# Two one-column operations for a half-mean, and another order of two adds, in a fused spectral convolution kernel

## The reference

```python
def L0(x):                                   # applied to _gn(x)
    X = jnp.fft.rfftn(x, axes=(-2, -1))
    Yr = rconv(Xr, wr) - rconv(Xi, wi) + b_real
    Yi = rconv(Xr, wi) + rconv(Xi, wr) + b_imag
    return jnp.fft.irfftn(lax.complex(Yr, Yi), axes=(-2, -1))
x = x + L0(_gn(x))
x = x + mean_filter_15x15(_gn(x))
```

## Time and profile before

| | |
|---|---|
| median of 3 runs | 4029.41 us (4027.86 to 4030.45) |
| the profiled execution | 4030.95 us |
| its span | 4028.9 us |
| PE busy | 3515.2 us (87%) |
| DVE busy | 3445.0 us (86%) |
| POOL busy | 2638.3 us (65%) |
| ACT busy | 2382.8 us (59%) |
| mean granted clock of TensorE | 0.962 |

### The profile page before, as it was taken

One profiled execution on the slowest core, in us unless ns is written; L12 is line 12 of the kernel. 1 busy time (PEld: TensorE's weight loads), 2 busy tenths in 40 slices (PEclk: granted clock), 3 DMA queues, 4 the chain that ended last, 5 costly groups with the idle time before them and its releaser, 6 DMA issues.

```text
span 4028.9 us, 122552 instructions
## 1 busy us (share of the span) xinstructions
PE 3515.2 (87%) x42592; PEld 2538.7 (63%) x42592; DVE 3445.0 (86%) x6382; ACT 2382.8 (59%) x3774; POOL 2638.3 (65%) x2177
## 2 busy tenths in 40 slices
PE   3199889998999989899798998999898998999988
PEld 1166576665766667666675666666576665766667
DVE  7889977998779978899788997789977998789976
ACT  0078733886248852588427883288733886248852
POOL 5088853887538865588546885388853986538865
PEclk8599999999999999999999999999999999999999
DMA  6511166111741128311382114711165111741114
GB/s 161 169 43 53 44 173 178 52 53 34 225 135 52 52 57 245 91 51 52 100 239 57 51 53 141 208 45 53 42 184 167 52 52 38 222 134 51 52 53 137
DMA packets 228530, 407.91 MB, mean 101 GB/s; under 512 B 98160, under 2 KB 173520, under 8 KB 215888
## 3 DMA queue, kind: packets, MB, share of 16 engines
q1 hardware_dynamic: 205776, 285.88, 24.6%
q10 hardware_dynamic: 22400, 117.46, 10.9%
HBM read 256.31 MB, written 146.80 MB: 100 GB/s over the span
## 4 chain that ended last, share of the span: by engine, by line
PE 52%; DVE 21%; issue 11%; POOL 8%; ACT 5%; ACTq 1%; DVEq 1%; SPq 1%; DMA 0%; POOLq 0%
PE h_ps L658 14%; PE p L549 11%; PE h_ps L453 9%; PE p L684 6%; PE p L491 4%; POOL ob_all L1306 3%; DVE arena L1104 3%; DVE ob_all L1152 3%; DVE half_row L1171 3%; PE xt_ps L443 3%; DVE img L1161 2%; POOL ob_all L1308 2%; POOL arena L1299 2%; DVE ob_all L1231 2%; ACT arena L727 1%
## 5 line engine op out<-in xcount | busy, mean ns | idle before, releaser
L549 PE MATMUL p<-arena,bd_all 64*64 64x512 f16 x16896 | 1206.4, 379 | 30.0 <-DVE ob_all L1152 29.6
L1299 POOL TENSOR_TENSOR arena<-arena 128x512 f16<-128x512 f32 x512 | 594.1, 1160 | 495.7 <-ACT arena L760 476.2
L453 PE MATMUL h_ps<-hilbert,arena 128*128 128x256 f16 x6144 | 754.5, 272 | 115.8 <-DVE arena L1104 111.9
L549 PEld LDWEIGHTS p<-arena,bd_all 64*64 64x64 f16 x16896 | 604.4, 106 | 385.6 <-issue 38.8
L453 PEld LDWEIGHTS h_ps<-hilbert,arena 128*128 128x128 f16 x6144 | 564.0, 97 | 398.7 <-issue 317.9
L1357 POOL TENSOR_TENSOR arena<-img 128x512 f32<-128x512 f32 x392 | 499.0, 1274 | 469.4 <-PE h_ps L658 443.9
L727 ACT ACTIVATE arena<-h_ps 128x512 f16<-128x512 f32 x512 | 305.7, 597 | 841.4 <-PE h_ps L658 593.9
L1308 POOL TENSOR_TENSOR ob_all<-ob_all,img 128x512 f32<-128x512 f32 x512 | 662.7, 1294 | 75.6 <-POOL ob_all L1306 60.6
L1306 POOL TENSOR_TENSOR ob_all<-ob_all 128x512 f32<-128x512 f32 x512 | 655.8, 1281 | 52.5 <-DVE ob_all L1152 51.9
L766 ACT ACTIVATE arena<-xt_ps 128x1024 f16<-128x1024 f16 x512 | 520.7, 1017 | 35.5 <-PE xt_ps L443 35.5
L658 PE MATMUL h_ps<-bd_all,arena 128*128 128x128 f32 x3584 | 539.5, 286 | 0.0
(11 more groups left out here) (163 smaller groups left out, 4980.6 us busy)
## 6 DMA issues: line engine op xcount, KB each, us to landing
out<-ob_all SPq DMA_DIRECT2D x512, 256.0 KB, 4.2
bd_all<-bd_dram SPq DMA_DIRECT2D x512, 192.0 KB, 2.3
img<-in_x ACTq DMA_DIRECT2D x168, 512.0 KB, 7.3
img<-in_x ACTq DMA_DIRECT2D x112, 256.0 KB, 4.8
wrap_mat<-tab_wrap_h SPq DMA_DIRECT2D x512, 32.0 KB, 2.0
img<-in_x SPq DMA_DIRECT2D x24, 512.0 KB, 23.1
bd_dram<-ob_all SPq DMA_DIRECT2D x16, 768.0 KB, 3.5
img<-in_x SPq DMA_DIRECT2D x16, 256.0 KB, 7.2
```

The source lines that it names most:

```text
L453: m = mm(dst(a), xT[:, 4 * lx + k, 0:rows], tb["hilbert16"][:, lt, k, 0:cols], start=(half == 0 and i == 0), stop=(half == 1 and i == 2))
L549: m = mm(bank[out_half * HP:(out_half + 1) * HP, :], bd[s % RB][rows, 6 * lm + (j if own else j + 1), :], part, start=opens and i3 == 0, s ...
L1299: G.tensor_tensor(gp[s][:, 1, :], g32, gp[s][:, 0, :], ALU.subtract).then_inc(g_split, 1)
```

## The change

`half_mean` makes the two values of half_row in two operations of one column, each with one tensor input, the constant -0.5 and `known` as a per-partition scalar, in place of one operation of two columns with two tensor inputs. `add_terms` on POOL first adds the image row and the cosine term t1, for which it waits for t1_done, and then the sine term t2, for which it waits for t2_done; the semaphore between the two adds is now called first_added. DVE, before it overwrites the term rows, waits for q_done of two rows back where it waited for t_added of the same row.

```diff
@@ wave_terms (DVE)
                     if first * NG + s > 1:
-                        dve.wait_ge(t_added, PRIMED + n - 1)
+                        dve.wait_ge(q_done, PRIMED + n - 1)
                     dve.wait_ge(p1_ready, n + 1)
@@ half_mean (DVE)
                     dve.wait_ge(x1_counted, n + 1)
-                    V.scalar_tensor_tensor(half_row[:, s, :], stat[:, t, 1:6:3], -0.5, known[:, t, :],
-                                           ALU.mult, ALU.add).then_inc(half_made, 1)
+                    for a in range(2):
+                        ins = V.tensor_scalar(half_row[:, s, a:a + 1], stat[:, t, 1 + 3 * a:2 + 3 * a], -0.5,
+                                              known[:, t, a:a + 1], ALU.mult, ALU.add)
+                    ins.then_inc(half_made, 1)
@@ add_terms (POOL)
                         pool.wait_ge(x1_done, PRIMED + n - 1)
+                    pool.wait_ge(t1_done, PRIMED + n + 1)
+                    G.tensor_tensor(q, term_row[s % 2][0], parity(img[:, t, :]), ALU.add).then_inc(first_added, 1)
+                    pool.wait_ge(first_added, PRIMED + n + 1)
                     pool.wait_ge(t2_done, PRIMED + n + 1)
-                    G.tensor_tensor(q, term_row[s % 2][0], term_row[s % 2][1], ALU.add).then_inc(t_added, 1)
-                    pool.wait_ge(t_added, PRIMED + n + 1)
-                    G.tensor_tensor(q, q, parity(img[:, t, :]), ALU.add).then_inc(q_done, 1)
+                    G.tensor_tensor(q, q, term_row[s % 2][1], ALU.add).then_inc(q_done, 1)
```

More of the change, by code:

```diff
@@ L254, in build @@
         p1_ready, p2_ready, p0_ready = sem("p1_ready"), sem("p2_ready"), sem("p0_ready")
-        t1_done, t2_done, t_added, q_done, x1_done = (sem("t1_done"), sem("t2_done"), sem("t_added"), sem("q_done"),
+        t1_done, t2_done, first_added, q_done, x1_done = (sem("t1_done"), sem("t2_done"), sem("first_added"), sem("q_done"),
                                                       sem("x1_done"))
@@ L964, in _ @@
                                          tb["hb_mask16"][:].rearrange("p (s c h) -> p s c h", s=2, h=HL), ALU.mult))
-            for primed in (t1_done, t2_done, t_added, q_done, x1_done, g_split, xt_kept, h_made, h_split, p0_ready,
+            for primed in (t1_done, t2_done, first_added, q_done, x1_done, g_split, xt_kept, h_made, h_split, p0_ready,
                            row_out, *stored):
```

## The result

| | before | after |
|---|---|---|
| median us (runs, lowest to highest) | 4028.64 (4, 4022.97 to 4030.45) | 3931.69 (4, 3929.96 to 3935.54) |
| span of the profiled execution | 4028.9 | 3931.1 |
| DVE busy us | 3445.0 | 3276.0 |
| PE busy us | 3515.2 | 3503.6 |

The ratio is 0.9763, with a 95% interval of 0.9746 to 0.9780: 97 us less. 3944 was forecast, in a range of 3926 to 3985.

What follows compares the result with a forecast made beforehand. DVE was taken to bound the kernel at 4.43 us a row, then PE at 4.20. 10.4 + 0.5 - 0.3 = 10.6 us an image, 85 in 8, took the median 4029.41 to 3944, range 3926 to 3985.

Steps and rivals of the forecast that it cites:

- The 4.18: Short L453 step in the middle of layer 0, read as PE's time for a row when it waits for nothing.
- DVE sets the step: Middle of layer 0, kernel before: DVE was said to bound the step of 4.43 us, with PE just behind.
- The sum 3.64 + L1171: DVE's time for a row in layer 0: 3.64 us without L1171, plus L1171, held until POOL lets go.
- PE is late next: Layer 0's rows after the change: PE was said to bound them at 4.20 us, saving 10.4 us an image.
- The pair: The two one-column half_row operations on DVE: forecast free of POOL, 0.14 us together.
- The presum rows: The ten or so rows where POOL presums the image's first rows: POOL is full, so they keep their step.
- The end of an image: Last rows: L1206 starts 0.9 us sooner, L1007 is then held; about 0.5 us gained, bounds 0 and 1.3.
- POOL's order: POOL's first add waits for t1_done alone: gain about nothing, its extra queue wait costs 0.3 us an image.
- part one: Half-mean on DVE: 512 two-tensor L1171 replaced by 1024 one-column tensor_scalar operations, taken to run free of POOL.
- (a): Rival: POOL holds the one-column form too; 4055 us, or 4490 if the second operation misses the gap; chance 0.08.
- (b): Rival: only part arrives, 0.65 us in the loops leaves DVE a step of 4.3; 3982 us, chance 0.08.
- (c): Rival: nothing measurable, DVE freed from L1171 waits in L1161 for POOL's q; 4029 us, chance 0.02.

Runs made afterwards that it cites:

- e8: Kernel before without the low part of the Hilbert matrix, 8 matmuls for 12 at L453: 3952.0 us, ratio 0.9814 to the kernel before.
- e10: Kernel before without ACT's second L783, so the half-mean isn't added to the odd columns: 3952.7 us, ratio 0.9817 to the kernel before.
- e7: Changed kernel without the low part of the Hilbert matrix, 8 matmuls for 12 at L453: 3922.2 us, ratio 0.9746 to the kernel before.
- e5: Changed kernel with one more pair of one-column operations a row, into a tile nobody reads: 3938.3 us, ratio 0.9776 to the kernel before.
- e3: Changed kernel with the half-mean as one tensor_scalar of two columns with one tensor input: 4022.8 us, ratio 0.9993 to the kernel before.
- e4: Changed kernel with the half-mean as two one-column operations with two tensor inputs each: 4039.5 us, ratio 1.0026 to the kernel before.
- e1: Changed kernel with POOL's adds in the old order, only the two one-column operations kept: 3936.2 us, ratio 0.9780 to the kernel before.

## Why the prediction came out as it did

**The time**: 85 us less were forecast, 97 measured, inside the range. The direction and the main part came from the right place: L1171 is freed, and the row then costs what the next bound has. 4.20 was taken for it, 4.195 measured. That these agree so well is in part luck. The 4.18 was read as a step in which PE waits for nothing, but L453 starts 0.16 after L1104's end in it (311.09 + 0.67 and 311.92), just as in the long step (0.15). PE's own sum is the 4.15 of the earlier trace rows; with it the forecast would have been 18 us lower, and what fills the 0.05 is a ring that the prediction doesn't have.

**"DVE sets the step"** is the step of the working that was wrong. The sum 3.64 + L1171 was true of every row, but L1171 wasn't a term of its own: e8 and e10 make it 0.2 shorter (627 and 604 ns for 830) without touching DVE. The bound was the two-row ring through PE, ACT and POOL, with L1171 as the link that closed it. It made no difference to the forecast, since the change cuts this very link. Had the question been what a faster ACT or PE is worth in the kernel before, the same working would have said nothing, and it is 75 us.

**"PE is late next"** was wrong for the looped rows. PE is busy 199.54 of 200 in the changed kernel, but its own sum is 4.15, and the ring through L549, L1146 and L1152 has 4.20; e7 takes 0.43 of PE's work away and most of these steps stay. In the rows that are written out on DVE, the presum rows and the very last ones apart, PE sets the step.

**The pair**: 0.14 was taken from L1023, 0.24 came (303.43 to 303.67). L1023 has constants alone. The form with a [P,1] scalar takes 204 ns for 154; e5 shows that there was room for that. That it is free of POOL was right in all 1024 cases, and L1146 was the right line to go by. e3 and e4 show that its one tensor input was not the whole reason, which the prediction left to the Trainium skill's rule.

**The presum rows** kept their steps of 4.95, as said. The extra wait on POOL's queue was put at 0.3 an image; nothing of it is to be seen in these steps.

**The end of an image**: 0.5 was forecast, 0.57 measured, with L1007 held as foreseen (1.00).

**POOL's order** was put at nothing, and 0.3 an image was taken off for its extra wait; with part one it is worth 0.8 an image (2.6 in e1, 1.80 with both), 6.6 us by the traces and 8.9 by the medians. With the 0.3 this is most of the 12 us between forecast and result. The error is in "for the very last row POOL is in L1319 until about the time t2 is ready": it is so before, but the adds of the row before move forward too, and L1319 and the last adds with them. The step moved one operation and left those behind it in place.

**The rivals**: (a) didn't come, and e4 has its price, 10 us where 25 were given; (b) wanted 0.65 for the pair, it was 0.24, and e5's 0.48 still passes; (c) is refuted by the absence of any wait of L1161 for POOL in the middle.

## What to carry to other kernels

A short operation that stands many times its own length beside another engine is no cost of its engine but a link between two: follow the chain through it, also over two steps, before the engine's busy time is called a bound. Alternating step lengths were the sign of a ring over two steps here. The value of freeing it is read from steps that wait for nothing; compare each start with the end of what it could wait for, since a small wait need not show as idle time. Each ring of nearly the same length has to be looked for by itself. And an earlier start on one engine can hold up a short operation on another: POOL's new order alone made L1171 take 0.90 where it had taken 0.15.

## What was not expected of the hardware

- A tensor_scalar of one column, one SBUF tensor and a [P,1] scalar ran beside POOL in 196 to 211 ns in all 1024 cases; with two columns it was held (837 ns in the loops), and so was one column with two SBUF tensors (1.11 us for a pair).
- The [P,1] scalar costs a one-column operation about 0.05 us: 204 ns against 154 with constants.
- Of two held operations in a row only the first was held (1.04 us, then 0.15); a split into two such ones cost a step 0.03 to 0.04 us, less than one operation's 0.07.
